# The last phase of a fused two-layer kernel: two turns of rows on TensorE set behind the down products of their step

## The reference, cut to what matters

```python
x = x + tanh(g_xattn[0]) * attention(layernorm(x), ctx)
x = x + tanh(g_ffn[0])   * experts(layernorm(x))          # shared expert and the best 2 of 8
x = x + tanh(g_xattn[1]) * gate(layernorm(x), ctx)
x = x + tanh(g_ffn[1])   * ffn(layernorm(x))

def gate(x, h):
    gate_x = sigmoid(block_diag_linear(x, w_input, b_input))
    gate_a = sigmoid(block_diag_linear(x, w_a, b_a))
    log_a = -8.0 * softplus(a_param) * gate_a
    a = exp(log_a)
    normalized_x = x * gate_x * sqrt(1.0 - exp(2.0 * log_a))
    return a * self_att_pool(h) + normalized_x

def ffn(x):                                               # 256 -> 1024 -> 256
    hidden = fwht(silu(x @ W1.T) * (x @ W3.T))
    return hidden @ W2.T
```

## Time and profile before

| | |
|---|---|
| median of 3 runs | 1432.47 us |
| profiled execution: its own time, its span | 1434.49 us, 1432.8 us |
| PE busy over the span | 1334.9 us, 93% |
| DVE, ACT, POOL busy | 925.9, 756.2, 686.2 us |
| mean granted TensorE clock | 0.969 |
| last phase, step 0 to the end | 1107.03 to 1432.8 us |

### The profile page before, as it was taken

How to read it: one execution, slowest core, us unless ns; L and a number is a source line. 1 busy time by engine, 2 the same in 40 slices (tenths; PEclk the granted TensorE clock), 3 DMA queues, 4 the chain that set the end, 5 groups by cost and what they waited for, 6 DMA issues and landing times. The chain is left out here.

```text
span 1432.8 us, 31669 instructions
## 1 busy us (share of the span) xinstructions
PE 1334.9 (93%) x9954; PEld 1017.8 (71%) x9955; DVE 925.9 (65%) x1689; ACT 756.2 (53%) x1461; POOL 686.2 (48%) x853
## 2 busy tenths in 40 slices
PE   4899999999999589998998999999987999999998
PEld 3555555555555268887877888888876788888887
DVE  7799999999997278766554333333335766665553
ACT  0477777777778544432342333333426656665642
POOL 7577777777772156443675223310044554445210
PEclk9999999999999789999999999999976999999999
DMA  3222222222221122114732333241131110111000
GB/s 103 79 81 83 79 88 82 73 86 85 78 73 38 51 83 80 60 59 138 238 124 82 97 97 95 67 142 51 45 96 41 30 44 28 34 45 30 15 16 30
DMA packets 85891, 105.53 MB, mean 74 GB/s; under 512 B 11249, under 2 KB 76145, under 8 KB 85425
## 3 DMA queue, kind: packets, MB, share of 16 engines
q1 hardware_dynamic: 75344, 70.38, 15.5%
q0 software_dynamic: 10464, 34.09, 7.5%
HBM read 53.05 MB, written 23.99 MB: 54 GB/s over the span
## 5 line engine op out<-in xcount | busy, mean ns | idle before, releaser
L469 ACT ACTIVATE e_t<-st_ps 128x512 f32<-128x512 f32 x512 | 278.5, 597 | 105.5 <-PE st_ps L557 101.9
L407 DVE TENSOR_REDUCE row_max<-s_ps 128x4 f32<-128x1024 f32 x256 | 311.3, 1218 | 21.8 <-PE s_ps L562 19.5
L584 PE MATMUL o_ps<-e_t,v_st 128*32 128x256 f32 x2048 | 166.5, 398 | 0.1
L557 PE MATMUL st_ps<-q_st,k_st 32*128 32x256 f32 x1024 | 160.5, 333 | 6.2 <-DMA q_st<-m_rows 3.6
L562 PE MATMUL s_ps<-k_st,q_st 32*128 32x256 f32 x1024 | 158.1, 342 | 5.1 <-DVE row_max L407 3.5
L557 PEld LDWEIGHTS st_ps<-q_st,k_st 32*128 32x128 f32 x1024 | 106.1, 187 | 56.0 <-issue 36.3
L1773 POOL DMA_INDIRECT gathered_tail<-sorted_results,result_at x64 | 70.8, 1106 | 125.3 <-POOLq L2299 107.2
L1640 PE MATMUL y_ps_moe<-w_all_moe,xt_hi_moe 128*128 x568 | 116.5, 286 | 7.7 <-DVE xt_lo_moe L1440 7.7
L2039 DVE TENSOR_TENSOR h_all_tail<-silu_tail,u_ps_tail 128x512 f32<-128x512 f32 x64 | 43.8, 685 | 118.7 <-ACT silu_tail L1888 64.5
L1446 DVE TENSOR_TENSOR h_all_moe<-silu_moe,u_ps_moe 128x512 f32<-128x512 f32 x71 | 48.8, 687 | 109.3 <-PE u_ps_moe L1609 109.3
L1124 ACT COPY y_sb_moe<-y_ps_moe 128x256 f32<-128x256 f32 x71 | 26.5, 373 | 162.2 <-PE y_ps_moe L1640 162.2
(11 more groups left out here) (341 smaller groups left out, 3613.7 us busy)
## 6 DMA issues: line engine op xcount, KB each, us to landing
k_st<-k_part SPq DMA_DIRECT2D x96, 128.0 KB, 2.1
q_st<-q_part SPq DMA_DIRECT2D x96, 128.0 KB
stage_moe<-in_experts POOLq DMA_DIRECT2D x21, 512.0 KB, 4.2
rows_in_moe<-sorted_rows SPq DMA_DIRECT2D x71, 128.0 KB, 2.0
sorted_results<-y_sb_moe SPq DMA_DIRECT2D x71, 128.0 KB, 1.7
c_in<-in_ctx SPq DMA_DIRECT2D x32, 128.0 KB, 2.2
x_sb<-in_x SPq DMA_DIRECT2D x32, 128.0 KB, 2.1
xn_moe<-in_ctx SPq DMA_DIRECT2D x8, 512.0 KB, 4.4
```

Of the source, the lines that this page charges most:

```text
L407: nc.vector.tensor_reduce(out, s_ps[p % 2][:], AX_X, ALU.max).then_inc(s["max_taken"], 1)
L469: nc.scalar.activation(e_t[t % 4][:, b, :, :], st_ps[:, b, :, :], ACT.Exp, scale=float(DH) ** -0.5)\
L557: last = nc.tensor.matmul(out, w, moving, start=True, stop=True)
L584: last = nc.tensor.matmul(o_ps[32 * j:32 * j + 32, :], values[:, at:at + 32], e_t[(2 * u + j // 2) % 4][:, j % 2, half_, :], start=(half_ ...
```

## The change

The gate turn at m=4 and the ffn turn at m=7 are issued behind the chunk's down products, where before they stood in front of them. The ffn turn moves only where a group st+2 exists (steps 0 to 5); in step 6 it stays in front. Nothing else changes, on any engine: the same instructions with the same waits, in another order on PE.

```diff
                 for m in range(CHUNKS):
                     products(st, m)
-                    if m == 4 and is_group(st + 2):
-                        turn("gate", st + 2)
                     if m == 5 and is_group(st + 1):
                         turn_back(st + 1)
-                    if m == 7 and is_group(st + 1):
+                    if m == 7 and is_group(st + 1) and not is_group(st + 2):
                         turn("ffn", st + 1)
                     if m >= 2:
                         if st == 0 and m == 2:
...
                         down(st, m - 2)
                     if m < 2 and is_group(st - 1):
                         down(st - 1, CHUNKS - 2 + m)
+                    if m == 4 and is_group(st + 2):
+                        turn("gate", st + 2)
+                    if m == 7 and is_group(st + 1) and is_group(st + 2):
+                        turn("ffn", st + 1)
                 if is_group(st + 2):
                     gates(st + 2)
```

## The result

The changed kernel took 1423.55 us (median of 4 runs, 1419.53 to 1424.58) against 1432.59 for the kernel before in the same comparison: ratio 0.993, 95% interval 0.9912 to 0.9948. A second set of runs gave 0.9934 (0.9914 to 0.9953). Both intervals lie clear of 1, and the gain is under 1%: 9.5 to 10 us by the two ratios, 9.0 and 8.2 by the medians, where 7.4 was forecast. The median itself, 1423.55, lies at the lower end of the stated range of 1423.2 to 1427.6; the ratio, 0.993 of 1432.59 or 1422.6, lies a little under it.

A forecast was written before the change was run, and what follows sets the result against it. PE's stream was taken to bound the phase, so only its waits on xn could be won: 2.3 + 4 x 1.11 + 0.61 = 7.4 us, from 1432.47 to 1425.1 us. Range: 1423.2 to 1427.6.

The forecast's parts named there:

- What bounds the phase: Steps 0 to 5: PE's own stream bounds; reordering can return only its idle time, 7.9 us in 10 waits on xn.
- Gate turn: Steps 1 to 5: down products fill the wait on xn, 0.61 us gained each; `turn_back` not held by ACT's copies.
- rival D: Gate turn: `turn_back` waits for ACT's late copies out of the shared `t_ps`; slower, 1445 us; chance 0.02.
- The gathers: POOL, steps 1 to 4: low part moves onto gather 4's start; xn 0.32 us late, gain 1.11 a step.
- The term for the hold: POOL, steps 1 to 4: gather 4, held by the rest of DVE's low part, ends up to 0.6 us late.
- the term for the small POOL operation: Behind the gathers: it took 0.52 us beside a low part that will now be over; half may come back.
- upper bound of 1.50 a step: Steps 1 to 4: the gain if nothing is held, the 0.52 is halved and PE itself is the limit.
- Rival A: POOL, steps 1 to 4: no gather is held; gain 8.8 us, 1423.7 us; chance 0.27.
- Step 0: Down products fill the wait at the gate turn and the clock holds; gain 2.3 us, bounds 1.4 and 3.0.
- rival B: Step 0: the clock falls all the same; gain 1.4 us there, 6.5 in all, 1425.9 us; chance 0.12.
- the 1.11: Steps 1 to 4: forecast gain in us per step for both turns, with xn taken 0.32 late.

The follow-up runs named there:

- the early rstd: Kernel before, PE's order untouched, with POOL taking the ffn's rstd after 6 of its 8 gathers instead of after all; ratio 0.9979.
- the version with the long memset: Changed kernel with a 128x256 POOL memset between gathers 3 and 4 of each step; 1429.87 us in one execution.
- the filling products: Kernel before with 10 products of 512 columns put ahead of the gate turn of step 0; ratio 1.0001.

## Why the prediction was right or wrong

- **What bounds the phase: right.** PE's stream, and with it the ten waits on xn; eight are gone and two are left in step 0 (1.38 and 0.45 shown, forecast 1.5 and 0.5). That xn of the ffn rows was late by POOL's queue is shown by the early rstd.
- **Gate turn: right.** `turn_back` came 3.67 us after the turn (1167.71 to 1171.38), forecast 3.73. ACT's copies did not hold it; rival D did not occur. (The last copy in the earlier trace rows reads 0.60, not "0.58 at most"; the bound would be 1173.98, still ahead of 1174.22.)
- **The gathers: wrong, and this is the step that failed.** "Held by the rest of it, gather 4 ends up to 0.6 late ... I take xn 0.32 late". The mechanism is real (gathers 1 and 3; gather 4 in the version with the long memset), but the two starts were a tie, and gather 4 got through. The term for the hold, 0.6, measured 0; the term for the small POOL operation, 0.26 given back, measured 0.27. So xn came 0.31 earlier after the step's start and not 0.32 later (1181.92 - 1146.47 = 35.45, before 1185.01 - 1149.25 = 35.76, forecast 36.1), the turn waited for nothing, and PE itself was the limit, which the prediction had as its upper bound of 1.50 a step. Rival A, to which the prediction gave 0.27, is what happened. The error of judgement was to take one side of a tie that I had named as one, and to let the range end 0.5 us past the other side's 1423.7: my own upper bounds add up to 3.0 + 4 x 1.50 + 0.61 = 9.6, or 1422.9, under the range's 1423.2.
- **A turn's own cost: missed by 0.06 us, twice a step in steps 1 to 4.** A turn behind a wait takes 0.85 to the next instruction (1142.44 to 1143.29), one without 0.79 (1182.16 to 1182.95). I carried the 0.85 over. With the two the bound of 1.50 a step becomes 1.62; measured 1.61. Step 5 had no wait at its ffn turn before, so it gets this once: 0.69 instead of 0.61. Over steps 1 to 5 it is about 0.5 us.
- **Step 0: right.** 2.30 forecast and measured. xn came 35.84 us after the step's start, forecast 1142.9 - 1107.03 = 35.87; that the gain agrees to the hundredth is luck, as it was forecast as 2.3 to 2.4. The clock held over a wait of 1.38 us (1.00 throughout the step), so rival B did not occur. B's 1.5 us for the slow stretch is what the filling products gave back there (1.55), though 3.9 us "costing half of it" would be 1.9: the clock was low for a part of it only.
- **The sum.** Forecast 2.3 + 4 x 1.11 + 0.61 = 7.4; measured 2.30 + 4 x 1.61 + 0.69 = 9.4. All but 0.1 of the difference lies in the 1.11. Between the two profiled executions another 0.5 us lies ahead of step 0 and has nothing to do with the change.

## What to carry to other kernels

Where two waits of one step hang on a chain that starts with the step, removing the first alone moves it to the second (2.8 us for one, 3.7 for the other, 9.4 for both): find what the second is released by before a gain is counted. Put the in-order work that others wait for (here a small rstd) ahead of bulk issues on the same queue, and independent products between a late operand's arrival and its first use. When two starts on engines that disturb each other lie within a tenth of a microsecond, price both outcomes and let the range hold both with room on either side.

## What the runs showed of the hardware

A gather's record is 0.94 to 0.97 us, and in these profiles it is longer only if the gather starts while DVE runs an operation with two SBUF operands; then it ends 0.8 to 1.1 us after that operation's end: 2.12 beside a sum of 1.23 that began 0.07 earlier, 1.32 at 0.20 after the start of a low part of 0.69. Another operation of DVE doesn't do it: in step 1 of the kernel before a gather that started at 1176.31, 0.02 into the update, which reads one of its operands from PSUM, took 0.95. One that starts first is not lengthened by what DVE starts later, and hardly lengthens it (0.72 or 0.73 for the low part in the tie, 0.68 or 0.69 without one). That is the gather's doing and not POOL's in general: a low part that started while POOL ran `scale` (step 6 of the kernel before, 1366.86) took 0.94. Where gather 4 and the low part start within 0.01 us of each other the gather got through every time: 24 times, in steps 1 to 4 of six profiles. The Trainium skill, "SBUF — State Buffer", "Who interferes with whom", has the loser blocked for the whole of the other's instruction; the trace bears that out where DVE is first and not where the gather is.

The granted clock stayed at its full level, 2.4 GHz, over a wait of 1.38 us and the transposes behind it, and over 0.46 with transposes; it fell to a mean of 0.51, its lower level of 1.2 GHz, behind a wait of 2.79, and filling 2.33 of that wait with products kept it at 1.00. The Trainium skill, "TensorE: Matmul & The Clock Gate", Part 4, doesn't count transposes as busy; here they never brought the clock down by themselves, which is no test of the rule.
